# Scores of one tile in two bursts, with the transposes of the tile before between them

## The chip, the cores and the metric

The kernel runs on one core of one Trainium2 chip. The metric is device time in microseconds (us). The core has TensorE for matrix products (PE; its weight loads are a row of their own, PEld), VectorE (DVE), ScalarE (ACT), GpSimd (POOL) and SyncE (SP), which here only issues DMAs. Each engine runs its own program in order, and the engines are tied by semaphores.

## The reference

The input is a sequence of 2048 vectors of 128. It goes through a half-weighted transformer stack, a Mamba block, and the same stack again. The stack is where nearly all the time is:

```python
for i in range(DEPTH):                                   # 6 layers
    x = attn_layer(shift_tokens(x), Wqkv[i], ...) + x    # 16 heads of 64, windows of 32
    x = ffn_layer(shift_tokens(x), ...) + x              # 341 hidden, gated by gelu

# in attn_layer, after q and k are normalised and rotated:
sim = einsum('bhwie,bhwje->bhwij', bq, bk2) * QK_SCALE   # 32 queries against 64 keys
sim = where(mask, -finfo.max, sim)
attn = softmax(sim, -1)
out = einsum('bhwij,bhwje->bhwie', attn, bv2)
```

The whole is `x + 0.5*stack(norm(x))`, then `x + mamba(norm(x))`, then `x + 0.5*stack(norm(x))`.

## The kernel before, in words

A tile is 128 tokens (four windows of 32). A layer has 16 tiles, a stack 6 layers, so n runs over 96 tiles in a stack, and there are two stacks: 192 tiles. All of it is one software pipeline written out by hand. Each engine has a loop over steps s; in step s, TensorE works on different stages of different tiles: the k projection of tile s-19, the out projection of s-23, the q transposes of s-20, the value products of s-22, the k transposes of s-20, the q projection of s-18, the v projection of s-20, the scores of s-20, and the transposes of the probabilities P of s-21. No scheduler moves anything: the order of the calls in the loop is the order on the engine, and every dependence is a semaphore wait.

Which lines are which on TensorE: L214 to L216 are one projection (three products of split float32 for each half, six per tile, `project`); L282 is eight transposes (of q, of k or of P); L359 is the eight mask products that start the scores' PSUM; L349 is one of the 64 score products of a tile, which the profile shows as 128 records since float32 takes two passes; L404 is a value product; L424 the out projection; L341 the carried keys; L447 and L467 the centring and variance products of the feed-forward part; L546 its down product.

A score product uses a 64x32 piece of the array. For each of eight head pairs there are four windows and two halves, so eight of them stand side by side, and a burst of them is 128 weight loads and 128 products. The projections, the transposes and the feed-forward products use the full 128x128 array.

PSUM is handed out by slots of 1024 columns. Slot 3 holds the scores of a tile and then its value products. Slot 2 holds in turn the q transposes, the v projection and the transposes of P. So `p_transpose(s-21)` waits for two things: that GpSimd has normalised P (L1768, semaphore `p_nrm`), and that ScalarE has copied this step's v projection out of slot 2 (L949, semaphore `v_ev`):

```python
pe.wait_ge(p_nrm, n0 + n + 1)
s = n + 21
after_tile(pe, v_ev, s - 20)
```

Around the scores: VectorE waits for `S_done`, takes the row maxima (L1357), later subtracts them (L1365); ScalarE takes the exponentials (L990); VectorE sums them (L1372) and takes reciprocals (L1376); GpSimd multiplies (L1768). The value products of the tile before (L404) go into slot 3, so they wait for the subtraction. After the transposes of P, ScalarE copies them out (L1004, two operations of 64 partitions) and squares k (L928).

Every four steps there are two plain steps, one with the centring and variance products (n % 4 == 2, called the centre step here) and one with the down products (n % 4 == 3, called the down step). In the down step VectorE adds the residual (L1465, L1467) once the down products are done, ahead of the row maxima. In the last down step of five layers of each stack it then also makes the low part of the next layer's W1 (L1283).

Of the kernel before, what the change touches and what calls it, by code (L numbers as in the profile page):

```python
# [16 lines left out]
N = NT * NL  # L17
# [14 lines left out]
def build(nc, xT, consts, wqkv, wo, w1, w2, lpar, qks, mpar, in_w, xp_w, dt_w, out_w, out):  # L32
    ctx = ExitStack()
    with ctx:
# [3 lines left out]
        def sem(name):  # L38
            return ctx.enter_context(nc.semaphore("s_" + name))
# [32 lines left out]
        def heads(ap, n=H):  # L72
            return ap.rearrange("p (h d) -> p h d", h=n)
# [60 lines left out]
        def unit(u):  # L134
# [27 lines left out]
        S_done, mx_done, sub_done, exp_done, sm_done, ri_done = (sem(n + "_done") for n in (  # L162
            "S", "mx", "sub", "exp", "sm", "ri"))
# [30 lines left out]
        def var_in(pe, r, c):  # L194
            pe.wait_ge(i_sq, 4 * r + c + 1)
            nc.tensor.matmul(PS[:, c, 512:1024], onesd, SXI[c], start=True, stop=True).then_inc(i_var, 1)

        def tensor_stack(pe, r):
# [46 lines left out]
            def k_project(n):  # L245
                if not 0 <= n < N:
                    return
                if n == 1:
                    keep_clock(3, 4)
                    pe.wait_ge(k_rot, n0 + 1)  # L250
                    project(1, 1, 1, k_done)
                    return
                pe.wait_ge(x_lo, N // 4 * r + n // 4 + 1)
                pe.wait_ge(w_lo[1], l0 + n // NT + 1)
                if n == 0:
                    pe.wait_ge(i_done, 4 * r + 2)
                    project(0, 1, 1, k_done)
                    return
                s = n + 19
                after_tile(pe, q_rot, s - 19)  # L260
                if s < RAMP or s >= N:
                    after_tile(pe, k_rot, s - 20)
                project(n, 1, 0, k_done)
# [79 lines left out]
            def score_tiles(n, pairs, slot=3):  # L343
                q, kt = heads(QT[n % 2], 8), by_pairs(KT[n % 2])
                for hp in pairs:
                    for win in range(4):
                        for par in range(2):
                            a, b, c = 64 * par, 64 * par + 64, 512 * par + 64 * hp
                            last = nc.tensor.matmul(  # L349
                                PS[32 * win:32 * win + 32, slot, c:c + 64], q[a:b, hp, 32 * win:32 * win + 32],  # L350
                                kt[a:b, hp, 32 * win:32 * win + 64], start=False, stop=True, skip_group_check=True)
                return last
# [8 lines left out]
                            MK[a:b, 64:128].unsqueeze(1).broadcast_to([64, 8, 64]), start=True, stop=False,  # L361
                            skip_group_check=True)

            def scores(n):
                if not 0 <= n < N:
                    return
                pe.wait_ge(qT_ev, n0 + n + 1)
                pe.wait_ge(kT_ev, n0 + n + 1)
                pe.wait_ge(car_ev, n0 + n + 1)
                if n == 0:  # L370
                    pe.wait_ge(i_done, 4 * r + 4)
                    if r == 0:
                        pe.wait_ge(masks_set, 1)
                s = n + 20
                if (s - 24) % 4 == 3:
                    after_chunk(pe, f_h[1], (s - 24) // 4)
                after_tile(pe, oT_ev, s - 22)
                if s < RAMP or s >= N:
                    after_chunk(pe, f_h[1], (s - 23) // 4 - 1)
                    after_tile(pe, sub_done, s - 21)  # L380
                score_masks(n)
                score_tiles(n, range(8)).then_inc(S_done, 1)

            def p_transpose(n):
                if not 0 <= n < N:
# [184 lines left out]
            def finish_tiles():  # L570
                def tile(sem, n):
                    pe.wait_ge(sem, n0 + n + 1)

                def units(sem, u):
                    pe.wait_ge(sem, c0 + u + 1)

                u = UNITS - 3
                tile(k_nrm, 95)
                tile(k_rot, 95)
                transposes(0, KN[1], kT_done)  # L580
                tile(oT_ev, 92)
                tile(res_done, 91)
                units(f_ln, u)
                out_products(92, 2)
                tile(q_nrm, 95)
                tile(PT_ev, 93)
                transposes(2, QN[1], qT_done)
                tile(sub_done, 94)
                pe.wait_ge(v2_in[1], 160 * ((n0 + 93) // 2 + 1))
                value_products(93)  # L590
                tile(qT_ev, 95)
                tile(kT_ev, 95)
                tile(car_ev, 95)
                score_masks(95, 0)
                score_tiles(95, range(8), 0).then_inc(S_done, 1)
                project(95, 2, 2, v_done)
                tile(oT_ev, 93)
                tile(res_done, 92)
                out_products(93, 2)
                tile(p_nrm, 94)  # L600
                transposes(3, P, PT_done)
                units(f_lo, u)
                tile(sub_done, 95)
                up_products(u, 1, 0)
                tile(res_done, 93)
                units(f_xm, u)
                up_products(u, 2, 2)
                tile(v_ev, 95)
                up_products(u, 0, 4)
                tile(PT_ev, 94)  # L610
                pe.wait_ge(v2_in[0], 160 * ((n0 + 94) // 2 + 1))
                value_products(94)
                tile(p_nrm, 95)
                units(f_h[1], u)
                transposes(0, P, PT_done)
                for j in range(3):
                    units(f_h[j], u)
                down_products(u, 3)
                centre_product(u + 1, 4)
                tile(oT_ev, 94)  # L620
                out_products(94, 2)
                units(f_sq, u + 1)
                variance_product(u + 1, 5)
                tile(PT_ev, 95)
                pe.wait_ge(v2_in[1], 160 * ((n0 + 95) // 2 + 1))
                value_products(95)
                if r == 0:
                    norm_mean(pe, 0, 1)
                    units(f_done, u)
                    norm_mean(pe, 1, 3)  # L630
                tile(oT_ev, 95)
                tile(res_done, 94)
                out_products(95, 2)
                units(f_lo, u + 1)
                up_products(u + 1, 0, 0)
                tile(res_done, 95)
                units(f_xm, u + 1)
                centre_product(u + 2, 4)
                if r == 0:
                    pe.wait_ge(m_xc, 1)  # L640
                up_products(u + 1, 1, 1)
                units(f_sq, u + 2)
                units(f_ln, u + 1)
                variance_product(u + 2, 5)
                if r == 0:
                    norm_variance(pe, 0, 2)
                    norm_variance(pe, 1, 7)
                    pe.wait_ge(m_xc, 2)
                else:
                    units(f_done, u)  # L650
                up_products(u + 1, 2, 3)
                units(f_ln, u + 2)
                if r == 0:
                    norm_mean(pe, 2, 5)
                else:
                    keep_clock(5, 7)
                units(f_lo, u + 2)
                up_products(u + 2, 0, 6)
                if r == 0:
                    pe.wait_ge(m_lnr, 2)  # L660
                up_products(u + 2, 1, 7)
                up_products(u + 2, 2, 2)
                units(f_h[0], u + 1)
                if r == 0:
                    norm_variance(pe, 2, 0)
                if r == 0:
                    pe.wait_ge(m_xc, 3)
                down_products(u + 1, 5)
                units(f_xm, u + 2)
                down_products(u + 2, 4)  # L670
# [18 lines left out]
            for s in range(115):  # L689
                if s == 19 + 1:  # L690
                    var_in(pe, r, 3)
                k_project(s - 19)
                out_project(s - 23)
                q_transpose(s - 20)
                values(s - 22)
                k_transpose(s - 20)
                ffn_up0(s - 24)
                ffn_up1(s - 24)
                ffn_up2(s - 24)
                q_project(s - 18)  # L700
                v_project(s - 20)
                scores(s - 20)
                carry(s - 19)
                ffn_centre(s - 23)
                ffn_down(s - 24)
                p_transpose(s - 21)
                ffn_variance(s - 23)
# [1363 lines left out]
```

## Time and profile before

| | us |
|---|---|
| median of 3 runs | 3296.12 |
| lowest and highest | 3295.41, 3300.77 |
| profiled execution, its own time | 3295.41 |
| profiled execution, span of the trace | 3293.6 |
| of the span, TensorE busy | 3128.0 (95%) |
| VectorE, ScalarE, GpSimd busy | 2773.5, 2490.9, 2435.9 |

The span is 1.8 us shorter than the execution's own time. A busy share is an average over stages; what bounds a step is read from the timeline of that step. "issue" as a releaser means that the engine waited for nothing that the profile shows. Where a duration is shown for a group of overlapping matmuls, it runs from the first start to the last (modelled) end. A mean granted clock of 1.00 in a stretch means TensorE ran at the upper of its two levels there.

### The profile page before, as it was taken

The numbers are of one execution on the slowest core, as the hardware profiler recorded it, in microseconds if no ns is written. First come the engines' busy times: TensorE is split into PE (matmuls) and PEld (weight loads), VectorE is DVE, ScalarE is ACT, GpSimd is POOL, SyncE is SP. The second block draws the span as 40 slices with busy tenths as digits, with TensorE's granted clock in tenths as the row PEclk, the third lists the DMA queues.
The fourth block names the chain that finished last, engine by engine and source line by source line (L and its number), as shares of the span: only waits on it lengthen the run. The fifth ranks groups of instructions, "written<-read, shape, count | busy, mean of one in ns | idle before, by whom it ended". The sixth has DMA issues, their size and how long they took to land.

```text
span 3293.6 us, 120453 instructions
## 1 busy us (share of the span) xinstructions
PE 3128.0 (95%) x51630; PEld 2513.7 (76%) x51630; DVE 2773.5 (84%) x3207; ACT 2490.9 (76%) x3160; POOL 2435.9 (74%) x1229
## 2 busy tenths in 40 slices
PE   7999999999999999998888999999999999999999
PEld 5887887888887887875333888888888888888777
DVE  7887888888888888876999888888888888888886
ACT  5777777777777787777676777778778777778776
POOL 6777777777777776762999868768768768768764
PEclk8999999999999999999999999999999999999999
DMA  3333333233233232231000323323323323323322
GB/s 119 88 76 86 77 85 87 72 89 87 68 92 85 70 89 66 67 76 38 26 0 0 98 67 82 88 71 85 91 69 83 95 69 81 96 66 83 73 66 68
DMA packets 142299, 245.22 MB, mean 74 GB/s; under 512 B 32397, under 2 KB 34638, under 8 KB 141774
## 3 DMA queue, kind: packets, MB, share of 16 engines
q1 hardware_dynamic: 141774, 237.51, 28.4%
q8 instruction: 415, 6.80, 0.9%
q14 instruction: 110, 0.90, 0.1%
HBM read 35.01 MB, written 1.05 MB: 11 GB/s over the span
## 4 chain that ended last, share of the span: by engine, by line
PE 83%; DVE 6%; issue 5%; POOL 3%; ACT 2%; DMA 0%; SPq 0%; DVEq 0%; ACTq 0%; POOLq 0%
PE PS L282 16%; PE PS L404 12%; PE PS L424 8%; PE PS L349 8%; PE PS L214 7%; PE PS L216 7%; PE PS L215 7%; PE PS L546 4%; PE PS L488 2%; PE PS L490 2%; PE PS L489 2%; PE PS L359 2%; POOL ARENA L1862 2%; PE PS L447 2%; DVE ARENA L1675 2%
## 5 line engine op out<-in xcount | busy, mean ns | idle before, releaser
L282 PE MATMUL PS<-C,ARENA 128*128 128x128 f32 x4608 | 619.7, 278 | 37.9 <-ACT ARENA L1004 11.4
L1746 POOL TENSOR_TENSOR ARENA<-ARENA 128x1024 f32<-128x1024 f32 x192 | 470.0, 2448 | 240.1 <-DVE ARENA L1325 239.2
L1754 POOL TENSOR_TENSOR ARENA<-ARENA,RN 128x1024 f32<-128x1024 f32 x192 | 365.3, 1903 | 371.4 <-ACT RN L939 371.4
L282 PEld LDWEIGHTS PS<-C,ARENA 128*128 128x128 f32 x4608 | 512.2, 141 | 119.4 <-issue 77.4
L1004 ACT ACTIVATE ARENA<-PS 64x1024 f32<-64x1024 f32 x384 | 390.5, 1017 | 181.3 <-PE PS L282 179.1
L214 PE MATMUL PS<-WL,XH 128*128 128x512 f32 x1152 | 498.8, 433 | 8.8 <-POOL XL L1713 4.0
L1740 POOL TENSOR_TENSOR ARENA<-ARENA 128x1024 f32<-128x1024 f32 x192 | 455.9, 2375 | 7.0 <-DVE ARENA L1307 7.0
L216 PE MATMUL PS<-WH,XH 128*128 128x512 f32 x1152 | 453.8, 394 | 0.0
L215 PE MATMUL PS<-WH,XL 128*128 128x512 f32 x1152 | 451.3, 392 | 0.0
L404 PE MATMUL PS<-ARENA 128*64 128x64 f32 x12288 | 402.4, 224 | 37.9 <-DVE ARENA L1365 22.2
L404 PEld LDWEIGHTS PS<-ARENA 128*64 128x64 f32 x12288 | 377.1, 138 | 72.5 <-issue 72.5
L1768 POOL TENSOR_TENSOR ARENA<-ARENA,RI 128x1024 f32<-128x1024 f32 x192 | 365.6, 1904 | 47.8 <-DVE RI L1376 30.2
L424 PEld LDWEIGHTS PS<-ARENA 128*128 128x128 f32 x3072 | 371.8, 192 | 18.9 <-issue 1.8
L1762 POOL TENSOR_TENSOR ARENA<-ARENA,RN 128x1024 f32<-128x1024 f32 x192 | 374.3, 1949 | 2.9 <-ACT RN L939 2.9
L424 PE MATMUL PS<-ARENA 128*128 128x128 f32 x3072 | 374.2, 275 | 1.1 <-ACT ARENA L1013 1.1
L1298 DVE TENSOR_TENSOR ARENA<-PS,TAB 128x1024 f32<-128x1024 f32 x192 | 235.0, 1224 | 148.4 <-ACT ARENA L915 148.4
L349 PE MATMUL PS<-ARENA 64*32 64x64 f32 x24576 | 293.1, 224 | 23.2 <-issue 23.0
L349 PEld LDWEIGHTS PS<-ARENA 64*32 64x32 f32 x24576 | 281.7, 105 | 41.7 <-issue 31.2
L1013 ACT ACTIVATE ARENA<-PS 128x1024 f32<-128x1024 f32 x192 | 196.8, 1025 | 125.0 <-PE PS L404 124.9
L1316 DVE TENSOR_TENSOR ARENA<-PS,TAB 128x1024 f32<-128x1024 f32 x192 | 234.3, 1220 | 50.6 <-ACT ARENA L928 50.6
L915 ACT ACTIVATE ARENA<-PS 128x1024 f32<-128x1024 f32 x192 | 197.1, 1026 | 90.1 <-PE PS L216 88.9
L214 PEld LDWEIGHTS PS<-WL,XH 128*128 128x128 f32 x1152 | 219.0, 190 | 58.9 <-issue 18.1
(160 smaller groups left out, 6454.4 us busy)
## 6 DMA issues: line engine op xcount, KB each, us to landing
ARENA<-ARENA SPq DMA_DIRECT2D x1152, 128.0 KB, 2.4
ARENA<-ARENA SPq DMA_DIRECT2D x768, 64.0 KB, 2.1
ARENA<-in_wqkv SPq DMA_DIRECT2D x36, 512.0 KB, 5.2
ARENA<-in_wo SPq DMA_DIRECT2D x12, 512.0 KB, 3.9
ARENA<-in_w SPq DMA_DIRECT2D x12, 341.0 KB, 3.2
ARENA<-in_w SPq DMA_DIRECT2D x12, 192.0 KB, 3.9
X<-in_xT SPq DMA_DIRECT2D x4, 256.0 KB, 5.5
out<-X SPq DMA_DIRECT2D x1, 768.0 KB, 3.6
```

Source lines behind the costliest of these rows:

```text
L214: nc.tensor.matmul(o, XH[:, x], WL[:, s], start=True, stop=False)
L215: nc.tensor.matmul(o, XL[:, x], WH[:, s], start=False, stop=False)
L216: last = nc.tensor.matmul(o, XH[:, x], WH[:, s], start=False, stop=True)
L282: last = nc.tensor.transpose(PS[:, slot, 128 * j:128 * j + 128], src[:, 128 * j:128 * j + 128], ident)
L349: last = nc.tensor.matmul(PS[32 * win:32 * win + 32, slot, c:c + 64], q[a:b, hp, 32 * win:32 * win + 32], kt[a:b, hp, 32 * win:32 * win + ...
L404: last = nc.tensor.matmul(out.rearrange("p (a q) -> p a q", a=2)[:, :, col:col + 32], v2[:, win, hp, :], pt[:, hp, win, :], start=True, st ...
L424: last = nc.tensor.matmul(PSB[:, bank, 0:128], w[:, 128 * j:128 * j + 128], OTS[:, 128 * j:128 * j + 128], start=j == 0, stop=j == 7)
L1004: last = act.activation(blocks[a:b, :, par, :], PS[a:b, slot, :].rearrange("p (b q) -> p b q", q=32), ACT.Copy)
L1740: nc.gpsimd.tensor_tensor(QN[n % 2], QN[n % 2], P if n == 1 else T2, ALU.add).then_inc(q_add, 1)
L1746: nc.gpsimd.tensor_tensor(KN[n % 2], KN[n % 2], T2, ALU.add).then_inc(k_add, 1)
L1762: nc.gpsimd.tensor_tensor(a, a, bc(RN[:, n % 2, 16:32], 64), ALU.mult).then_inc(k_nrm, 1)
L1768: nc.gpsimd.tensor_tensor(heads(P), heads(P), bc(RI[:, n % 2, :], 64), ALU.mult).then_inc(p_nrm, 1)
```

## The change

The scores of a tile are issued in two parts. The masks and the products of head pairs 0 to 3 stay where they were. The products of head pairs 4 to 7, and with them the signal `S_done`, come at the head of the next step, which is behind the transposes of P of that step (and behind the carry, centring, down and variance products where the step has them) and ahead of the k projection. In the last step they stand at the head of `finish_tiles`.

```diff
-            def scores(n):
+            def scores_low(n):
                 if not 0 <= n < N:
                     return
...
                 score_masks(n)
-                score_tiles(n, range(8)).then_inc(S_done, 1)
+                score_tiles(n, range(4))
+
+            def scores_high(n):
+                if 0 <= n < N:
+                    score_tiles(n, range(4, 8)).then_inc(S_done, 1)
...
                 u = UNITS - 3
+                scores_high(94)
                 tile(k_nrm, 95)
...
             for s in range(115):
                 if s == 19 + 1:
                     var_in(pe, r, 3)
+                scores_high(s - 21)
                 k_project(s - 19)
                 out_project(s - 23)
                 q_transpose(s - 20)
...
                 v_project(s - 20)
-                scores(s - 20)
+                scores_low(s - 20)
                 carry(s - 19)
```

On TensorE, a plain step in the middle of the first stack, from the masks to the k projection, before. The names in brackets are the semaphores waited for ahead of an instruction; an x with a number is how often it stands in a row.

```order
L359 MATMUL PS<-MK 32x512 [waits s_car_ev,s_oT_ev,s_kT_ev,s_qT_ev]
L359 MATMUL PS<-MK 32x512 x7
L349 MATMUL PS<-ARENA 32x64 x64
L282 MATMUL PS<-C,ARENA 128x128 [waits s_v_ev,s_p_nrm]
L282 MATMUL PS<-C,ARENA 128x128 x7
L214 MATMUL PS<-WL,XH 128x512 [waits s_q_rot,s_w_lok,s_x_lo]
```

The same place now:

```order
L359 MATMUL PS<-MK 32x512 [waits s_car_ev,s_oT_ev,s_kT_ev,s_qT_ev]
L359 MATMUL PS<-MK 32x512 x7
L349 MATMUL PS<-ARENA 32x64 x32
L282 MATMUL PS<-C,ARENA 128x128 [waits s_v_ev,s_p_nrm]
L282 MATMUL PS<-C,ARENA 128x128 x7
L349 MATMUL PS<-ARENA 32x64 x32
L214 MATMUL PS<-WL,XH 128x512 [waits s_q_rot,s_w_lok,s_x_lo]
```

The eight transposes have moved ahead of 32 score products; the number of products is the same.

On TensorE, a centre step before, from the scores to the k projection (L447 is the centring product, L467 the variance product):

```order
L349 MATMUL PS<-ARENA 32x64 x64
L447 MATMUL PS<-ARENA,C 128x512 [waits s_kT_ev,s_res_done]
L282 MATMUL PS<-C,ARENA 128x128 [waits s_v_ev,s_p_nrm]
L282 MATMUL PS<-C,ARENA 128x128 x7
L467 MATMUL PS<-ARENA,C 128x512 [waits s_car_ev,s_f_sq]
L214 MATMUL PS<-WL,XH 128x512 [waits s_q_rot,s_w_lok,s_x_lo]
```

The same place now; the two products' lines have become L451 and L471:

```order
L349 MATMUL PS<-ARENA 32x64 x32
L451 MATMUL PS<-ARENA,C 128x512 [waits s_kT_ev,s_res_done]
L282 MATMUL PS<-C,ARENA 128x128 [waits s_v_ev,s_p_nrm]
L282 MATMUL PS<-C,ARENA 128x128 x7
L471 MATMUL PS<-ARENA,C 128x512 [waits s_car_ev,s_f_sq]
L349 MATMUL PS<-ARENA 32x64 x32
L214 MATMUL PS<-WL,XH 128x512 [waits s_q_rot,s_w_lok,s_x_lo]
```

The second half of the scores now stands behind the variance product and its wait for the square. The order on the other engines is as it was.

## Rows read from the trace of the kernel before

**Rows 1.** The page: busy time, the instruction queue, the chain by engine.
```profile
PE 3128.0 (95%) x51630; PEld 2513.7 (76%) x51630; DVE 2773.5 (84%) x3207; ACT 2490.9 (76%) x3160; POOL 2435.9 (74%) x1229
...
q8 instruction: 415, 6.80, 0.9%
...
PE 83%; DVE 6%; issue 5%; POOL 3%; ACT 2%; DMA 0%; SPq 0%; DVEq 0%; ACTq 0%; POOLq 0%
```

**Rows 2.** Stretches from masks to masks: length, then busy time of PE, PEld, DVE, ACT, POOL.
```profile
707.65:720.12 12.47, 12.47 (x260) 11.07 (x259) 11.80 (x15) 10.39 (x13) 11.71 (x7) 1.00 0.46 115
732.96:752.37 19.41, 18.73 (x281) 15.08 (x280) 15.45 (x19) 15.34 (x20) 15.53 (x8) 1.00 0.23 57
752.37:767.92 15.55, 15.55 (x268) 12.59 (x267) 12.89 (x16) 12.06 (x14) 11.52 (x6) 1.00 0.29 70
767.92:781.15 13.23, 12.70 (x261) 11.15 (x260) 11.31 (x14) 10.38 (x13) 11.64 (x7) 1.00 0.34 82
...
813.99:831.29 17.30, 15.64 (x269) 12.63 (x268) 15.17 (x17) 11.90 (x14) 9.61 (x5) 1.00 0.25 63
```

**Rows 3.** Timeline of a plain step: start, us, engine, line, operation, count.
```profile
707.11 1.90 POOL L1768 TENSOR_TENSOR ARENA<-ARENA,RI 128x1024 f32<-128x1024 f32 x1 [0.37 <-DVE RI L1376]
...
707.65 0.41 PE L359 MATMUL PS<-MK 64*32 64x512 bf16 x8
...
707.76 1.02 ACT L949 ACTIVATE ARENA<-PS 128x1024 f32<-128x1024 f32 x1 [0.34 <-PE PS L216]
707.88 1.46 PE L349 MATMUL PS<-ARENA 64*32 64x64 f32 x128
...
709.27 1.09 PE L282 MATMUL PS<-C,ARENA 128*128 128x128 f32 x8
...
710.12 0.47 PE L214 MATMUL PS<-WL,XH 128*128 128x512 f32 x1
...
710.85 1.21 DVE L1357 TENSOR_REDUCE MX<-PS 128x16 f32<-128x1024 f32 x1
...
713.37 1.04 PE L282 MATMUL PS<-C,ARENA 128*128 128x128 f32 x8
...
714.34 2.08 PE L404 MATMUL PS<-ARENA 128*64 128x64 f32 x64
```

**Rows 4.** The same timeline, window cut off at 708.5: the first half of the scores.
```profile
707.88 0.83 PE L349 MATMUL PS<-ARENA 64*32 64x64 f32 x65
```

**Rows 5.** Timeline of a centre step.
```profile
734.58 1.12 PE L447 MATMUL PS<-ARENA,C 128*128 128x512 f32 x2
...
735.74 0.60 ACT L1023 ACTIVATE ARENA<-PS 128x512 f32<-128x512 f32 x1 [0.79 <-PE PS L447]
736.15 1.21 DVE L1357 TENSOR_REDUCE MX<-PS 128x16 f32<-128x1024 f32 x1
...
736.41 1.10 PE L467 MATMUL PS<-ARENA,C 128*128 128x512 f32 x2
...
738.81 2.03 ACT L1004 ACTIVATE ARENA<-PS 64x1024 f32<-64x1024 f32 x2
738.94 0.69 DVE L1397 TENSOR_TENSOR ARENA<-PS,ARENA 128x512 f32<-128x512 f32 x1 [1.58 <-ACT ARENA L1035]
...
740.99 1.06 PE L282 MATMUL PS<-C,ARENA 128*128 128x128 f32 x8 [0.30 <-ACT ARENA L1004]
```

**Rows 6.** Timeline of the plain step that took 13.23 us.
```profile
767.72 1.22 DVE L1298 TENSOR_TENSOR ARENA<-PS,TAB 128x1024 f32<-128x1024 f32 x1 [0.86 <-ACT ARENA L915]
...
768.14 1.36 PE L349 MATMUL PS<-ARENA 64*32 64x64 f32 x117
...
770.04 0.33 PE L349 MATMUL PS<-ARENA 64*32 64x64 f32 x11 [0.53 <-issue]
770.04 0.17 PEld L349 LDWEIGHTS PS<-ARENA 64*32 64x32 f32 x10 [0.68 <-issue]
```

**Rows 7.** The waits: us in total, times, longest.
```profile
PEld PS L349 <- issue: 31.2, 52, 1.0
...
PE PS L404 <- DVE ARENA L1365: 22.2, 33, 1.7
```

**Rows 8.** Timeline of a down step in which VectorE makes W1's low part.
```profile
818.92 0.74 DVE L1465 SCALAR_TENSOR_TENSOR ARENA<-PS,LP,ARENA 64x512 f32<-64x512 f32 x1 [1.65 <-PE PS L546]
...
820.47 2.34 DVE L1283 TENSOR_TENSOR W1L<-ARENA,W1H 128x682 fp32r<-128x682 f32 x1
822.84 1.22 DVE L1357 TENSOR_REDUCE MX<-PS 128x16 f32<-128x1024 f32 x1
...
825.47 1.74 PE L404 MATMUL PS<-ARENA 128*64 128x64 f32 x52 [1.66 <-DVE ARENA L1365]
```

## The prediction

> **What bounds the kernel now.** I read the page first. TensorE is busy 95% of the span, and the chain that ended last runs over it for 83% [rows 1]. An average can hide stages with other limits, so I then cut the span from one mask product to the next, which is one step each, and read the busy time in each stretch [rows 2]. A clean plain step takes 12.47 us and TensorE is busy in all of them; so is a down step (15.55 of 15.55). A centre step takes 19.41 with 18.73 busy. So in plain and down steps each 0.1 us that TensorE gains or loses goes into the end, and other engines matter only where they make it wait.
>
> Two things stand out. The plain step that begins at 767.92 takes 13.23 us, 0.76 more than the clean one, with the same work [rows 2]. Its timeline shows why: the scores stop after 117 of 128 products, and nothing that the profile knows of releases them [rows 6]. The weight loader stood 0.68 us idle there while the step lost 0.76. The waits count 52 such stops of the loader inside L349, 31.2 us in all [rows 7]. And at the end of five layers a down step takes 17.30, because the value products wait 1.66 us for VectorE's subtraction [rows 2, 8].
>
> **What the stops are.** The scores are 128 loads and 128 products in 1.46 us [rows 3], by far the densest stretch of instructions. The instruction queue moved 6.80 MB in 415 transfers [rows 1], so 16 KB each, for 103,260 loads and products, so about 249 of them to a transfer. One burst of scores uses up about a whole transfer. A plain step has about two transfers' worth of instructions, so the border falls at nearly the same place in step after step and drifts slowly; that fits stops in some layers and none in others. I take the stops as TensorE running out of instructions. By the Trainium skill (Runtime: NRT & Kernel Launch, "Instruction fetch mechanics") instructions come in 16 KiB blocks of 256, which agrees with the size in the row; but the page also holds the crossing of a block to be "mostly hidden". By that, there would be nothing to win here; rows 6 show that it is not hidden.
>
> After the change a window of 256 instructions around the scores also holds the eight transposes, which take 0.85 us (709.27 to 710.12 [rows 3]), and the second half of the scores begins a good 2.2 us after the masks (below), where the stop of rows 6 had ended by 770.04, 2.12 after its masks at 767.92. So the instructions are there when the burst needs them. I count the 31.2 us and 0.08 more for each of the 52 (0.76 against 0.68), 35 us, and take back 34, as some may remain. Bounds: nothing, if the stops only move, and 37 (a few short ones at other lines).
>
> **A plain step, part by part.** Times are from the masks' start, 707.65 [rows 3].
> - The first half: the 65th product starts at 707.88 + 0.83 - 0.22 (one product's length) = 708.49 [rows 4], so the half takes 0.60 from 0.23 to 0.83. Before, the transposes started 0.15 after the last score's start (707.88 + 1.46 - 0.22 = 709.12, then 709.27). So the transposes could start at 0.98.
> - But they go into the PSUM slot that ScalarE empties with L949, which ends at 707.76 + 1.02, that is 1.13. Before, the whole burst of scores hid it, as the transposes came at 1.62. After a write of ScalarE, TensorE starts 0.07 later (L1023 ends 736.34, L467 starts 736.41) to 0.12 (L1004 ends 740.84, L282 starts 740.99) [rows 5]. So they start at about 1.23, a new wait of 0.25 us. Queued behind it are the second half of the scores, the k projection and all the rest. Bounds 1.20 and 1.28.
> - Eight transposes to the first product on a full array take 0.85; to products on a piece of the array they take 0.97 (713.37 to 714.34) [rows 3], so the switch costs 0.12. The 0.85 also holds a slow first transpose behind the scores, so I take 1.0. The second half starts at 2.23.
> - The second half takes between 0.50 (its instructions are queued up during the transposes) and 0.64 (1.24, all starts of the burst, less 0.60). I take 0.58, near the first half. Then 0.15 to the full array again. The k projection starts at 2.96, where it was 710.12, 2.47. That is 0.49 more per plain step; bounds 0.35 (1.20 + 0.97 + 0.50 + 0.15 = 2.82) and 0.62.
>
> Of this 0.25 is the wait and 0.24 the extra pair of array switches. The Trainium skill says the same against this change (TensorEngine Tiling (Array Packing), "Key Properties": changing the tiling mode drains the engine) without a price; the trace agrees with 0.12 on the way in and 0.15 on the way out.
>
> Does the later `S_done` cost? It comes at 2.23 + 0.58 + 0.22 = 3.03; VectorE gets to the row maxima at 710.85, 3.20, since it is busy with the rotations before. 0.17 us of cover is left. So the softmax behind it starts when it did, and P, which GpSimd has ready at 707.11 + 1.90 = 1.36 in this step, comes no later in the loop; since the step gets 0.49 longer and k is squared a little earlier, it is ready before 1.23 in the next.
>
> **Over the program.** 96 of 192 steps are plain; at the ends of the stacks some have no neighbour: 94 x 0.49 = 46 us (33 to 58).
> Down steps: the transposes come far behind L949, so only the switches count: 36 x 0.24 = 9 us (4 to 14).
> Ten down steps with W1's low part: VectorE starts behind the down products, which come 0.64 us earlier since half of the scores has gone from ahead of them; the row of VectorE operations up to the value products [rows 8] moves as a whole: 10 x -0.64 = -6 us.
> Centre steps: centring (L447, before at 734.58), square, transposes and variance come 0.64 earlier, so the variance product is at 735.77; its two passes last 1.10 to a modelled end that the next product does not quite wait for, which puts the second half at about 736.81, the maxima at 736.81 + 0.58 + 0.25 = 737.64, 1.49 later than before. They end at 738.85. VectorE then takes L1397, which before waited until 738.94 for ScalarE's L1035 [rows 5], and that is 0.64 earlier now. So the wait is filled by the late maxima, VectorE gains 0.1, and the value products, which wait for it, come 0.1 earlier. 48 x -0.1 = -5 us (-7 to +5).
> Instruction stops: -34 us.
> Sum: 46 + 9 - 6 - 5 - 34 = +10 us. The profiled execution's own time is 3295.4, so 3305; it lies 0.7 under the median of the runs, which changes nothing.
>
> **The rivals.**
> 1. The second half is cheap. If its instructions stand ready and the wait is 0.07, plain steps cost 33 us and down steps 4: 33 + 4 - 6 - 7 - 37 = -13, so 3283. For it: the first products of a burst do come faster than the later ones (0.60 and 0.64). Against: all of its terms must lie at their ends. Chance 0.20 for this side, from 3289.5 down.
> 2. It cancels: plain steps lose 0.40 and the stops give back 35. 38 + 7 - 6 - 5 - 35 = -1, so 3295. Chance 0.27.
> 3. The stops stay or move into the second half or the k projection. Then nothing is given back: +44, 3339. For it: what ends a stop has no name in the profile. Against: all 52 are in the densest burst, and the stretch of 256 instructions gets longer by nearly 1 us. The Trainium skill's Runtime page cited above ("mostly hidden") would lead here too, since by it the fetch has no price that could be won back. Chance 0.07.
> 4. The softmax loop binds. If `S_done` comes later than 3.20, each 0.1 us beyond moves the maxima, the subtraction and at last P; once P is later than 1.23 the transposes wait for it and `S_done` is later again. From 0.17 us more in the second half on, a plain step costs some 0.1 more: 3305 + 9 = 3314. For it: 0.17 is thin. Against: VectorE idles 0.86 ahead of L1298 in a plain step [rows 6], which takes such a delay up. Chance 0.06.
>
> **How the numbers follow.** About 0.2% (6.6 us) is what a measurement of this kernel can tell from no change. The forecast, 3305, has 0.40; with rivals 3 and 4 the slower side has 0.53. Rival 2 has 0.27 and rival 1 0.20. The range runs from 3287 to 3326: it takes in most of rivals 1 and 2 and, above, plain steps at 0.62 with a third of the stops left; it leaves out rival 3.
>
> **What would show it.** Right: in clean plain steps 12.9 to 13.0 us from masks to masks instead of 12.47; about 90 waits of TensorE at L282 for ScalarE's L949, 0.2 us or so each; no stops with the releaser "issue" inside L349; down steps near 15.8, the long ones near 16.7 instead of 17.30; maxima in plain steps still 3.2 after the masks. Wrong: plain steps at 12.6 to 12.7, then the switches and the wait are over-priced and the kernel is faster; stops that go on, then they are not what I take them for; maxima released by L349 in plain steps, then rival 4 holds.

## The result, and the profile after

The changed kernel is slower: 3330.93 us (median of 4 runs, 3329.32 to 3331.4) against 3297.36 for the kernel before (4 runs), a ratio of 1.0102 with a 95% interval of 1.0088 to 1.0116. The forecast was 3305 with a range of 3287 to 3326. The sign was right, the size was not: +10 forecast, +34 measured. The profiled execution took 3331.24, its span is 3329.5, that is 35.9 more than before. Below line 361 the lines of the changed kernel stand further down, by 4 for TensorE's (L404 is now L408, L424 is L428, L546 is L550) and by 6 for the other engines' (L949 is L955, L1283 is L1289, L1357 is L1363, L1365 is L1371).

The page after; the same parts as in [rows 1]:

```profile
PE 3179.2 (95%) x51630; PEld 2524.1 (76%) x51630; DVE 2793.2 (84%) x3207; ACT 2503.3 (75%) x3160; POOL 2435.9 (73%) x1229
...
q8 instruction: 415, 6.80, 0.9%
...
PE 79%; DVE 7%; issue 7%; POOL 4%; ACT 3%; DMA 0%; SPq 0%; DVEq 0%; POOLq 0%; ACTq 0%
```

The same number of instructions in the same number of transfers, and TensorE is busy 51 us longer. The span after, cut from masks to masks, to be read beside [rows 2]: a plain step, a centre step, a down step and one with W1's low part.

```profile
790.62:803.72 13.10, 12.89 (x259) 11.16 (x258) 11.31 (x14) 9.90 (x12) 10.39 (x6) 1.00 0.35 84
742.41:761.60 19.19, 18.99 (x281) 15.11 (x280) 15.23 (x19) 15.45 (x20) 15.29 (x8) 1.00 0.24 58
761.60:777.50 15.90, 15.90 (x267) 12.69 (x266) 12.90 (x16) 12.07 (x14) 12.17 (x6) 1.00 0.27 68
823.09:840.39 17.30, 16.05 (x268) 12.73 (x267) 15.79 (x17) 11.91 (x14) 9.61 (x5) 1.00 0.25 63
```

The clean plain step went from 12.47 to 13.10, the down step from 15.55 to 15.90; the one with W1's low part stayed at 17.30. The centre step shown is the one of [rows 2], 19.41 before; it is one of seven at 19.18 to 19.19 after, and most centre steps take 19.37. The timeline of that plain step (masks at 790.62) answers to [rows 3]:

```profile
788.93 1.90 POOL L1774 TENSOR_TENSOR ARENA<-ARENA,RI 128x1024 f32<-128x1024 f32 x1
...
790.72 1.02 ACT L955 ACTIVATE ARENA<-PS 128x1024 f32<-128x1024 f32 x1 [0.35 <-PE PS L216]
790.84 0.84 PE L349 MATMUL PS<-ARENA 64*32 64x64 f32 x64
...
791.89 1.06 PE L282 MATMUL PS<-C,ARENA 128*128 128x128 f32 x8 [0.21 <-ACT ARENA L955]
...
792.88 0.86 PE L349 MATMUL PS<-ARENA 64*32 64x64 f32 x64
...
793.67 0.50 PE L214 MATMUL PS<-WL,XH 128*128 128x512 f32 x1
...
793.80 1.21 DVE L1363 TENSOR_REDUCE MX<-PS 128x16 f32<-128x1024 f32 x1
```

Behind the masks the transposes start at 1.27 (forecast 1.23), the second half of the scores at 2.26 (2.23) and the k projection at 3.05 (2.96). The row maxima (L1363) begin at 3.18 without a wait, as before; of its 83 waits in the list below, 48 are in centre steps, 29 in down steps and 6, of 0.16 to 0.27 us, in plain steps. The waits after:

```profile
DVE MX L1363 <- PE PS L349: 92.9, 83, 5.8
PEld PS L349 <- issue: 59.0, 189, 0.8
...
PE PS L408 <- DVE ARENA L1371: 26.0, 46, 1.3
PE PS L282 <- ACT ARENA L955: 16.4, 84, 0.2
```

The 84 waits for ScalarE's v copy are there. The 189 of the loader inside L349 are no stops: they stand at the entry of each second half, 0.17 in a plain step; inside the bursts one gap of over 0.2 us is left of 53 (the 52 of [rows 7] and a short one). The steps of the kernel before took 36.8 us more than their clean lengths (28.1 in plain steps, 5.9 in centre and 2.7 in down steps). That came back. What it cost was more than forecast.

Not all of the 28.1 are stops. Ten plain steps, one in each of the first five layers of both stacks, took 12.80 to 13.11 us with no stop inside the scores. They hold the first q projection with the next layer's weights, and TensorE waits there for their low part, which GpSimd makes in L1722. In the kernel before, in the step that begins at 720.12:

```profile
727.92 2.00 POOL L1722 TENSOR_TENSOR WL<-ARENA,WH 128x1024 fp32r<-128x1024 f32 x1
...
730.00 0.19 PEld L214 LDWEIGHTS PS<-WL,XH 128*128 128x128 f32 x1 [0.33 <-issue]
```

L1722 ends at 729.92, and the first load starts at 730.00. After, the same operation ends at 739.13 and its load starts at 739.45, so nothing waits. This is 4.0 us of the 28.1, which the prediction did not have in its sum; about 33 us of the 36.8 are stops. e8 below tells the two apart: with the border moved, these ten steps still take 12.81 to 13.13.

Where the 35.9 of span are, as sums over all steps of a kind, before and after: plain steps 1125.0 and 1154.3 (88 steps), down steps 711.3 and 723.6 (44, the ten with W1's low part among them), centre steps 741.5 and 735.1 (38), all the rest +0.7.

### The profile page after: what moved, and what is told of

The parts are those of the page before. It is cut to its first block, busy times and chain, and to the rows that moved or that the text cites. A ratio compares the mean times of both kernels' runs of the same rounds, so it can differ in the third digit from the quotient of the medians.

```text
span 3329.5 us, 120453 instructions
## 1 busy us (share of the span) xinstructions
PE 3179.2 (95%) x51630; PEld 2524.1 (76%) x51630; DVE 2793.2 (84%) x3207; ACT 2503.3 (75%) x3160; POOL 2435.9 (73%) x1229
## 4 chain that ended last, share of the span: by engine, by line
PE 79%; DVE 7%; issue 7%; POOL 4%; ACT 3%; DMA 0%; SPq 0%; DVEq 0%; POOLq 0%; ACTq 0%
PE PS L282 15%; PE PS L408 11%; PE PS L428 8%; PE PS L214 8%; PE PS L216 7%; PE PS L215 7%; PE PS L349 6%; PE PS L550 4%; ACT ARENA L955 3%; PE PS L492 2%; PE PS L494 2%; PE PS L493 2%; POOL ARENA L1868 2%; PE PS L451 2%; DVE ARENA L1681 2%
## 5 line engine op out<-in xcount | busy, mean ns | idle before, releaser
L282 PE MATMUL PS<-C,ARENA 128*128 128x128 f32 x4608 | 615.0, 277 | 42.9 <-ACT ARENA L955 16.4
L282 PEld LDWEIGHTS PS<-C,ARENA 128*128 128x128 f32 x4608 | 512.9, 141 | 119.7 <-issue 76.4
L214 PE MATMUL PS<-WL,XH 128*128 128x512 f32 x1152 | 489.7, 425 | 7.3 <-POOL XL L1719 4.0
L1746 POOL TENSOR_TENSOR ARENA<-ARENA 128x1024 f32<-128x1024 f32 x192 | 457.3, 2382 | 7.0 <-DVE ARENA L1313 7.0
L408 PE MATMUL PS<-ARENA 128*64 128x64 f32 x12288 | 403.7, 224 | 42.0 <-DVE ARENA L1371 26.0
L408 PEld LDWEIGHTS PS<-ARENA 128*64 128x64 f32 x12288 | 378.7, 139 | 77.1 <-issue 77.1
L1304 DVE TENSOR_TENSOR ARENA<-PS,TAB 128x1024 f32<-128x1024 f32 x192 | 235.0, 1224 | 230.5 <-ACT ARENA L921 230.5
L428 PEld LDWEIGHTS PS<-ARENA 128*128 128x128 f32 x3072 | 372.2, 191 | 17.8 <-ACT ARENA L1019 1.5
L428 PE MATMUL PS<-ARENA 128*128 128x128 f32 x3072 | 373.7, 275 | 1.1 <-ACT ARENA L1019 1.1
L349 PEld LDWEIGHTS PS<-ARENA 64*32 64x32 f32 x24576 | 292.4, 105 | 69.3 <-issue 59.0
L349 PE MATMUL PS<-ARENA 64*32 64x64 f32 x24576 | 326.0, 223 | 0.1
L1363 DVE TENSOR_REDUCE MX<-PS 128x16 f32<-128x1024 f32 x192 | 234.2, 1220 | 94.8 <-PE PS L349 92.9
```

Of the source, the lines that this page charges most:

```text
L214: nc.tensor.matmul(o, XH[:, x], WL[:, s], start=True, stop=False)
L282: last = nc.tensor.transpose(PS[:, slot, 128 * j:128 * j + 128], src[:, 128 * j:128 * j + 128], ident)
L349: last = nc.tensor.matmul(PS[32 * win:32 * win + 32, slot, c:c + 64], q[a:b, hp, 32 * win:32 * win + 32], kt[a:b, hp, 32 * win:32 * win + ...
L408: last = nc.tensor.matmul(out.rearrange("p (a q) -> p a q", a=2)[:, :, col:col + 32], v2[:, win, hp, :], pt[:, hp, win, :], start=True, st ...
L428: last = nc.tensor.matmul(PSB[:, bank, 0:128], w[:, 128 * j:128 * j + 128], OTS[:, 128 * j:128 * j + 128], start=j == 0, stop=j == 7)
L1746: nc.gpsimd.tensor_tensor(QN[n % 2], QN[n % 2], P if n == 1 else T2, ALU.add).then_inc(q_add, 1)
```

## The experiments

All are timed in three rounds against the kernel before, which took 3294.83 us in the rounds of e1 to e4 and 3296.98 in those of e5 to e8. Theory A is mine each time. "Clean" is a step's length where nothing disturbs it.

**e1: six head pairs in the first part, two in the second.**

```diff
-                score_tiles(n, range(4))
+                score_tiles(n, range(6))
...
-                    score_tiles(n, range(4, 8)).then_inc(S_done, 1)
+                    score_tiles(n, range(6, 8)).then_inc(S_done, 1)
```

> The changed kernel with six head pairs ahead of the transposes of P and two behind, instead of four and four. Theory A: a plain step pays (1) a wait for ScalarE's copy of v out of PSUM slot 2, which ends 1.13 after the masks, and (2) one more pair of array switches. With six pairs ahead, the transposes could start at 0.22 + 0.91 + 0.15 = 1.28, just when the wait ends, so (1) goes from 0.29 to about 0, and the 32 products that are left behind are all queued up and take 0.24 instead of 0.64. Plain steps at 12.7 instead of 13.10, down steps at 15.8 instead of 15.90, no waits for L955 longer than 0.05, no stops inside the scores; time 3285 to 3297. Rival B (any split costs the same, by the switches alone): plain steps stay at 13.1, time 3331. Rival C (only the wait goes, the second burst costs per switch and not per product): plain steps 12.8, time 3304.

3307.08 (3303.99 to 3309.77), ratio to before 1.0033 (1.0019 to 1.0047). No wait of L282 for L955 is left. A plain and a down step:

```profile
782.59:795.35 12.76, 12.76 (x261) 11.08 (x260) 11.22 (x14) 9.99 (x12) 10.63 (x6) 1.00 0.35 86
754.00:769.83 15.83, 15.83 (x269) 12.60 (x268) 12.90 (x16) 12.06 (x14) 12.10 (x6) 1.00 0.28 68
```

Both are 0.28 to 0.29 above the clean steps of before, so an extra pair of array switches costs that much, with no wait. The clean steps are those of A, but the total came out 10 us above its band: the steps with W1's low part stayed at 17.30, the plain steps behind them took 12.95 (1.5 us in all), and 4.3 us lie in the centre steps of the last layers and 1.6 between the stacks; the cause of these two stays open.

**e2: two head pairs in the first part, six in the second** (`range(2)` and `range(2, 8)`).

> The changed kernel with two head pairs ahead of the transposes of P and six behind. Theory A: the transposes still start at 1.27 after the masks, since they wait for the copy of v, while the first burst is over at 0.68; the wait grows from 0.29 to 0.6 us and shows as TensorE idle at L282 for L955, some 0.5 in each of about 94 plain steps. Plain steps at 13.4, down steps 15.9 as in the changed kernel, time 3355 to 3362. Rival B (the cost is in the switches alone): plain steps stay at 13.1, time 3331.

3342.42 (3341.99 to 3344.28), ratio 1.0148 (1.0133 to 1.0163). A plain step, a down step and one with W1's low part:

```profile
793.66:807.08 13.42, 12.90 (x261) 11.18 (x260) 11.40 (x14) 9.98 (x12) 10.40 (x6) 1.00 0.33 82
764.34:780.25 15.91, 15.91 (x268) 12.69 (x267) 12.92 (x16) 12.06 (x14) 12.18 (x6) 1.00 0.29 68
826.46:842.38 15.92, 15.92 (x269) 12.69 (x268) 13.76 (x17) 12.00 (x14) 10.56 (x5) 1.00 0.27 68
```

```profile
PE PS L282 <- ACT ARENA L955: 45.6, 90, 0.5
```

The plain step is at A's 13.4, and 0.3 us more of it is wait than in the changed kernel, as the shorter first part hides less of ScalarE's copy. The total is 13 us below A's band. With e1 this settles the plain step: the extra pair of switches costs 0.28 to 0.37, by the down steps, which have no such wait, and the wait is 0, about 0.3 or about 0.6 (of which the profile shows 0.2 and 0.5 as idle time at L282). The miss lies in the last row: the step with W1's low part fell from 17.30 to 15.92. The ten of them took 18 us less than in the changed kernel (164.2 for 182.2), which I had not forecast. It showed where to look (e5).

**e3: the place of the 256-instruction border moved.** Into the kernel before, 44 tiny products are put once, ahead of the first loop; they write a piece of PSUM that nothing reads. Each is two loads and two products, 176 instructions in all.

```diff
+                for _ in range(44):
+                    nc.tensor.matmul(PSB[0:32, 7, 0:2], ident[0:32, 0:32], ident[0:32, 0:2], start=True, stop=True)
```

> The kernel before, with 44 tiny float32 products (176 loads and products) once at the very start, where TensorE waits anyway; nothing else is changed. Theory A: the 52 stops inside the scores are TensorE running out of instructions, and they come where the border of a 256-instruction block falls 205 to 275 instructions behind the masks. 176 more instructions move all later borders by that many, to 130 to 200 behind the masks, where the block was asked for early enough. Nearly all stops in plain and centre steps go; some short ones of 0.1 to 0.5 us come up in down steps. Time 3262 to 3275. Rival D (the stops have to do with what the steps work on, or with DMA traffic): they stay where they are, time 3297.

3286.52 (3280.88 to 3288.67), ratio 0.9974 (0.9965 to 0.9984): faster, with work added. The waits:

```profile
PEld PS L349 <- issue: 12.5, 22, 2.3
```

The step that had its stop in [rows 6] is clean, 12.47:

```profile
767.00:779.47 12.47, 12.47 (x260) 11.07 (x259) 11.38 (x14) 10.38 (x13) 11.57 (x7) 1.00 0.36 87
```

In the kernel before, all 53 stops stand at the same place of TensorE's instructions counted modulo 256 (193 or 194, with the waits for semaphores counted too), and so do all 22 here. Of the 63 steps in which that place comes 205 to 275 instructions behind the masks 48 have a stop, of the 129 others 5; so a stop nearly always has its border there, but a border there does not always make a stop. Shown: the stops belong to the border between blocks.

The transfers on the instruction queue, which the trace also has, say what a stop waits for. There are 415 of 16 KB, one for each border in TensorE's instructions. In the step of [rows 6], TensorE passed a border at 767.15, the next block's transfer started at 767.43 and took 1.36, and the scores went on at 770.04, 2.61 behind its start. All 53 stops end 2.3 to 2.9 us behind the start of the transfer before them, and in the whole trace no border was passed sooner than 2.2 us behind its transfer's start. So a stop comes where TensorE reaches the border before that.

The gain is smaller than A said (3262 to 3275), for 22 stops were left, and because one of them, at the start of the first stack, was 2.2 us long and cost more than itself (see the last section).

**e4: 64 tiny products, 256 instructions, a full turn.**

> Control for the moved border: 64 tiny products (256 loads and products), one whole block. Theory A: every border falls at the same place of a step as before, so the stops are where they were, 31 us of them at the loader inside L349, and the time is 3297 within 0.2%. If instead the tiny products themselves shift the start or anything else, this run shows by how much.

3298.07 (3294.2 to 3301.88), ratio 1.0006 (0.9997 to 1.0015), and 47 waits of the loader for 28.5 us as in [rows 7]. All stand at 193 or 194 again. So it is not the added products that help but the place of the border.

**e5: the kernel before, with W1's low part one step later.**

```diff
-                    w1_low(l + 1)
...
+                if 0 <= s - 25 < N - NT and (s - 25) % NT == NT - 1:
+                    w1_low((s - 25) // NT + 1)
```

> The kernel before, but VectorE makes the low part of the next layer's W1 (L1283) not behind the residual of the last down step, but one step later, between the two rotations of q. Before, the ten down steps with it take 17.30 us against 15.55 for the others. Theory A (what pins these steps is the chain of VectorE's L1283, 2.34 us there, and the maxima behind it, and the length of L1283 comes from GpSimd's L1740 beside it): these steps fall to 15.55 to 15.9, the plain step behind them has about 1.1 us of idle VectorE and takes L1283 at a cost of 0 to 0.5 us: 3279 to 3284 where the kernel before has 3295. Theory B (L1283 is worth its 2.3 us wherever it stands, since GpSimd is busy in every step): the plain steps behind get 1.2 us longer, 3289 to 3293. Theory C (these down steps are long for something else): 3295.

3281.01 (3279.37 to 3283.77), ratio 0.9952 (0.9937 to 0.9967). The down step that was 17.30 in [rows 2], and the plain step behind it, which now holds the operation:

```profile
811.30:826.84 15.54, 15.54 (x267) 12.58 (x266) 12.88 (x16) 11.88 (x14) 9.53 (x5) 1.00 0.28 70
826.84:839.94 13.10, 12.73 (x259) 11.09 (x258) 12.02 (x15) 10.39 (x13) 11.77 (x7) 1.00 0.34 83
```

and VectorE's and GpSimd's work there:

```profile
827.79 0.86 DVE L1283 TENSOR_TENSOR W1L<-ARENA,W1H 128x682 fp32r<-128x682 f32 x1
828.56 1.22 DVE L1307 TENSOR_TENSOR ARENA<-PS,TAB 128x1024 f32<-128x1024 f32 x1
828.60 1.90 POOL L1755 TENSOR_TENSOR ARENA<-ARENA,RN 128x1024 f32<-128x1024 f32 x1 [0.87 <-ACT RN L939]
```

The same operation takes 0.86 us where no GpSimd operation is running, 2.34 in [rows 8]. The total and the down steps are those of A: 1.75 off the one step, and 4.0 off in the fifth layer's. The next step pays 0.63, a little more than A's 0 to 0.5.

**e6: the changed kernel with the same move.**

> The changed kernel with the same move of the W1 operation as in e5. My prediction gave these ten steps 0.64 us each from the change, and they gave nothing, since VectorE's operation (L1289) started 0.62 earlier but ended at the same moment as GpSimd's L1746. Theory A: these steps fall from 17.3 (and 21.9) to the 15.9 of the other down steps (and about 20.4), 14 us less: 3317 where the changed kernel has 3331. Theory B: the same 3 to 6 us as B of e5: 3325 to 3328.

3309.26 (3308.0 to 3310.52), ratio to before 1.0038 (1.0024 to 1.0052), so 21.7 less than the changed kernel. Eight steps fell from 17.3 to 15.90, the two at 21.9 fell to 16.9. A had the eight right; it gave the two longest 20.4, and the total came out 8 us below its 3317. Against e5, which is the kernel before with the same move, the split of the scores costs 28 us here (3281.01 and 3309.26), and the stops that it takes away are in that sum.

**e7 and e8: the best of both.** The kernel before with e5's move, and 44 or 50 tiny products as in e3.

> The kernel before, with 44 tiny products ahead of the loop (176 instructions, as in e3) and the W1 operation later (as in e5). If the two are independent: 3286.5 (e3) less what e5 gains, so 3271 to 3275 by A of e5, 3281 to 3284 by B. A version that should beat both kernels.

> As e7, but with 50 tiny products (200 instructions) instead of 44. In e3 the 22 stops that were left were in down steps (12) and plain steps (10), all at the same place modulo 256 in TensorE's instructions, where the border comes 205 to 275 instructions behind the masks (170 to 290 in down steps, with shorter stops). 24 more instructions move the plain steps' border to 172 to 205 behind the masks, out of that region, and leave only down steps in it. Theory A (a stop is a late block of 256 instructions and depends on where the border stands in the step): no stop is left in plain steps, about 12 short ones in down steps, and it is 3 to 5 us faster than e7. Theory D (the number of stops varies with the layout for some other reason): no such order.

e7 took 3273.43 (3272.66 to 3276.96), ratio 0.993 (0.9916 to 0.9945), which is e3's gain and e5's added. e8 took 3271.23 (3269.62 to 3272.35), ratio 0.9921 (0.9906 to 0.9936). Of e7's 23 stops inside the scores 14 were in plain steps, of e8's 19 only 7, while those in down steps went from 6 to 9. That is A's order, but not its amount: A had none in plain steps and 3 to 5 us, and the 2 us between the two lie within the intervals, so a gain is not shown. In e8 the same place also shows as idle time of the loader behind the scores, 0.5 to 1.1 us long in three centre steps (at L447), which a count of the stops inside the scores leaves out. Both versions beat both kernels by 0.7% and more.

## Why the prediction was wrong

**The plain step, "0.49 more", was mis-sized: it is 0.63.** The mechanism was right in each part. By the timeline the transposes started 0.04 later than reckoned (1.27, a wait of 0.29 instead of 0.25): the sum allows 0.07 to 0.12 from ScalarE's end to TensorE's start, but its own second pair of times, 740.84 and 740.99, is 0.15 apart, and 0.15 is what it was (791.74 to 791.89). The second half took 0.64 and not 0.58 to the end of its starts, and the products behind it came another 0.05 later than my sum. The 0.58 was my choice between 0.50 and 0.64, on the ground that a burst's first products come faster; they do, but for a second half the full price was due. The step came out 0.01 above its upper bound, 0.62. Over the plain steps this is +56 instead of +46.

**The down step, "only the switches count", was right in kind and 0.11 short:** +0.35 for +0.24, +12 in all for +9. By e1 and e2, where the down steps have no new wait either, it is the pair of switches with the burst's second entry. The 0.24 came from the same sum, and 0.06 of what it lacks is the second half's price again. The Trainium skill (TensorEngine Tiling (Array Packing), "Key Properties") says that a change of the tiling mode drains the engine; e1, e2 and the changed kernel agree, with 0.28, 0.37 and 0.35 us for an extra pair.

**The step that failed in its mechanism is "the row of VectorE operations up to the value products moves as a whole: 10 x -0.64".** It and the mis-sized plain step are each 10 us of the 24 by which the sum was off. VectorE's residual did come 0.62 earlier behind the masks. But the operation behind it did not end earlier. After, masks at 823.09:

```profile
827.40 0.74 DVE L1471 SCALAR_TENSOR_TENSOR ARENA<-PS,LP,ARENA 64x512 f32<-64x512 f32 x1 [1.03 <-PE PS L550]
...
828.79 2.39 POOL L1746 TENSOR_TENSOR ARENA<-ARENA 128x1024 f32<-128x1024 f32 x1
828.95 2.96 DVE L1289 TENSOR_TENSOR W1L<-ARENA,W1H 128x682 fp32r<-128x682 f32 x1
831.14 2.53 POOL L1768 TENSOR_TENSOR ARENA<-ARENA,RN 128x1024 f32<-128x1024 f32 x1
831.94 1.22 DVE L1363 TENSOR_REDUCE MX<-PS 128x16 f32<-128x1024 f32 x1
```

and in e2, where VectorE comes first:

```profile
832.01 0.92 DVE L1289 TENSOR_TENSOR W1L<-ARENA,W1H 128x682 fp32r<-128x682 f32 x1
832.16 3.01 POOL L1746 TENSOR_TENSOR ARENA<-ARENA 128x1024 f32<-128x1024 f32 x1
832.96 1.22 DVE L1363 TENSOR_REDUCE MX<-PS 128x16 f32<-128x1024 f32 x1
```

L1289 stretches from 2.34 to 2.96, the 0.62 it had gained, and ends 0.73 us behind GpSimd's L1746, which ended at 831.18. Before, its end was also 0.73 behind GpSimd's (822.81 and 822.08, by rows of the same view). GpSimd's operation had not moved (5.71 behind the masks before, 5.70 after), and held it. In e2 VectorE started 0.15 us ahead of it and took 0.92, and it was GpSimd's that stretched, from 2.39 to 3.01. So the two don't slow each other in proportion: in these steps the one that started first ran through and the other waited. The Trainium skill has the rule (SBUF — State Buffer, "SBUF: two separate sides"): a VectorE operation with both inputs in SBUF and a GpSimd operation that reads SBUF share a port pair under an exclusive lock for the whole instruction. The traces agree with 0.86 and 0.92 against 2.34 and 2.96; I had not used it. These steps gave 0 for eight of them.

The other two, in the fifth layer of each stack, became longer, 21.90 and 21.99 for 20.87. TensorE waits over 3 us there for the subtraction, before (3.63) and after (3.27), and starts the value products 13.52 behind the masks in both. After, they run at a granted clock of 0.50, the lower of its two levels (1.2 of 2.4 GHz):

```profile
1331.40:1333.30 1.90, 1.84 (x35) 1.87 (x36) 1.86 (x4) 1.86 (x2) 0.00 (x0) 0.50 0.00 0
1333.30:1335.20 1.90, 1.90 (x36) 1.78 (x34) 1.90 (x3) 0.02 (x1) 0.98 (x1) 0.50 0.00 0
```

Before, the first 1.6 us of the same products had a granted clock of 0.86, and the burst took 2.79 instead of 3.68. Why the clock fell earlier after the change, no run here shows. So the term was +2 instead of -6. And the plain step behind each of the eight is 13.35, not 13.10, because P comes late there; in TensorE's row it is

```profile
841.88 1.09 PE L282 MATMUL PS<-C,ARENA 128*128 128x128 f32 x8 [0.43 <-POOL ARENA L1774]
```

which is another 2 us. e6, with the operation moved away, has 13.09 there.

**The centre step, -0.1 each, gave next to nothing.** In the step of [rows 5] the maxima started 4.83 behind the masks with a wait of 1.56 (forecast 4.68, again by the second half's price). There the subtraction came 0.23 earlier, the value products waited 0.20 where they had waited 0.38, and the step went from 19.41 to 19.19, more than forecast. But that step was a poor sample: in most others the subtraction came when it had, 8.06 behind the masks, and a clean step is 19.37 after and 19.36 before. What the centre steps gained, 6.4 us, is in the main the 5.9 of their stops.

**Instruction stops, -34, was right:** about -33. e3 with e4 and the transfers show that they are the border's. The wait for L1722 gave back 4 more, which is luck, as the sum did not have it. Rival 3 is out: in the changed kernel no plain step is longer by a stop. Rival 4 is out as well in plain steps, as their maxima wait for nothing in nearly all.

The sum with measured terms: 56 + 2 (behind the W1 steps) + 12 (down) + 2 (W1 steps) - 1 (centre) - 33 (stops) - 4 (wait for L1722) = +34, against a span that grew by 35.9. The range ended at 3326 since its upper end took the plain steps at 0.62 and a third of the stops left, but kept the -6 of the W1 steps, the -5 of the centre steps and the 9 of the down steps at their middle values; all three came out above them.

## What to carry to other kernels

Where an engine is busy nearly all the time, splitting a dense burst of small-tile products cost a pair of array switches each time (0.28 to 0.37 us here), and what the long burst had hidden became a wait; both can be estimated from the timeline before the change. Don't move a chain of operations "as a whole" on paper: look at what runs on GpSimd beside each VectorE operation with both inputs in SBUF, for here the operation that was held by it ended right behind it, however early it started. And look for stops with the releaser "issue" inside the densest stretch: if they stand at one place modulo 256 of the engine's instructions, a few idle instructions ahead of the loop move them. Look at where they go: in e3 and e8 some came up at the starts of the stacks, where they cost more.

## What the runs showed of the hardware that was not expected

**A late block of instructions is worth 1% here.** By the Trainium skill (Runtime: NRT & Kernel Launch, "Instruction fetch mechanics") instructions come in blocks of 256 and crossing one is "mostly hidden". The blocks agree; hidden it is not where a step's densest 128 products run into the border: 53 stops, about 33 us over the clean steps. With 176 idle instructions the kernel was 0.26% faster; with the changed order of the scores the stops were gone.

**A long stop costs more than its length.** In e3, just after the start of the first stack, TensorE stood 2.2 us in the scores, and the products behind it had a granted clock of 0.57:

```profile
84.81:88.61 3.80, 1.62 (x130) 1.40 (x129) 3.28 (x3) 1.46 (x3) 2.96 (x3) 1.00 0.53 187
88.61:92.59 3.98, 3.98 (x21) 3.37 (x21) 2.45 (x2) 1.40 (x2) 3.98 (x2) 0.57 0.68 164
```

That step took 17.03 instead of 12.95. The second stack's start has the same, in e8 with the loader idle for 2.95 and a step of 17.46:

```profile
1839.00:1842.20 3.20, 3.20 (x123) 2.51 (x123) 2.41 (x5) 2.49 (x4) 2.85 (x2) 1.00 1.00 399
1842.30:1845.30 3.00, 0.25 (x23) 0.09 (x10) 1.92 (x2) 0.32 (x1) 2.59 (x2) 0.97 0.37 96
1845.30:1849.00 3.70, 3.66 (x23) 3.12 (x24) 2.45 (x2) 0.71 (x2) 3.48 (x2) 0.57 0.69 167
```

The DMA engines were full (1.00, 399 GB/s) up to the moment at which it stopped. The block of instructions was late because its transfer started late, and not because it was slow: TensorE passed the border before at 1840.18, the transfer started only at 1843.00, took 1.06, and the scores went on at 1845.34. In the step of [rows 6] the transfer started 0.28 behind the border, here 2.82. That it was held up by the other traffic fits, but no run here tells it apart. With both starts clean, e8 would have some 8 us more to win, an estimate from the two longest steps (16.79 and 17.46 against 12.95).
